# Expert outputs of a two-layer model weighed in feature rows on one core

## The chip, the cores and the metric

The kernel runs on one core of a Trainium2 chip. The metric is the device time of one execution in microseconds (us). A core has TensorE (PE, matrix products into the PSUM memory), VectorE (DVE), ScalarE (ACT), GpSimd (POOL), SyncE (SP, here only a queue of DMAs) and 16 DMA engines. PE, DVE and ACT reach PSUM; POOL works on SBUF alone. Each engine runs its own list of instructions in order and waits on semaphores.

## The reference, cut to what matters

128 images become 65 tokens of 64 features each, and pass two blocks of attention (or recurrence) and a mixture of experts. Each of the two mixtures has 8 experts, of which every token takes two:

```python
combine = sum(topk_probs[..., None] * one_hot(topk_idx, E), axis=-2)      # layer 0
for e in range(E):
    h = relu(einsum('bsd,hd->bsh', x, W1[e]) + b1[e])
    y = einsum('bsh,dh->bsd', h, W2[e]) + b2[e]
    out = out + combine[..., e:e + 1] * y
...
weights = sum(tp[..., None] * one_hot(ti, NE), axis=1)                    # layer 1
for e in range(NE):
    hh = silu(flat @ w1[e].T) * (flat @ w3[e].T)
    out = out + weights[:, e:e + 1] * (hh @ w2[e].T)
```

The attention of layer 1 ends in `x = x + y @ wo.T`, then `x` is added to `h`.

## The kernel before, in words

`h` holds all tokens as [128 images, 65, 64]. `program` runs six phases one after another, with a barrier of all engines between them. Two of them are `moe(0, ...)` and `moe(1, ...)`; the last part of the attention of layer 1, just ahead of `moe(1, ...)`, is `output1`.

`moe` takes the 65 tokens in 13 groups of 5 (`T = 5`, so 640 columns of 5 tokens by 128 images). All experts are computed for all tokens. The first products have feature rows: a unit `u` is one block of 128 hidden features times half a group (320 columns), made of two matmuls in layer 0 (weights in a high and a low part, L1306) and of four in layer 1 (gate and up). Hidden features go from PSUM to `hid` through DVE or ACT (L1079, L1216 in layer 0; L1074 and then L1210 in layer 1). `down` (L1317) multiplies them by the second weights and gives `psY`, 64 features of two experts in 128 rows; ACT's `read_y` copies it to `y[slot][:, p, :]` (L1063, L1065), p = 0 to 3 being the pair of experts.

The order is written out by hand. `body(g, ...)` of each engine walks over places (p, k): pair p and the k-th unit of it, 8 units for each pair in layer 0 and 6, 6, 4, 6 in layer 1. Tables say at which place other work stands: `LOGITS` (router products of group g), `DOWN` (`down` of the pair before), `HI`, `KEEP`, `TURN` (the next group's normalised tokens transposed), `EXP`, and `SLOTS`, steps of DVE's small work: "a" and "e" routing of group g, "n" the norm of group g + 1. PE may run up to four units ahead of their eviction in layer 0 (`wait_evicted(pe, g, u - 4)`); in layer 1 gate products have three PSUM banks. `down(p)` waits for the eviction of all of pair p.

`OUTS` and `WEIGH` place the end of the group before: `token_major` (L1328) turns `y` back to image rows, 4 transposes of 128x128 for each token, 20 for each group. `weigh` on DVE (L1200) multiplies the 512 columns of a token by its 8 routing weights, out of PSUM. POOL's `add_up` adds 512 columns to 64 in three steps (L1001, L1003, L1004) and the sums to `h` (L1006). In layer 1 SP stores each group (L1026).

`output1` has 13 groups too. For each token `yT[:, at:at + B]` is the stationary matrix and `wo1`, 64 columns, moves through it (L1968). DVE adds the product to `x` (L1976) and `x` to `h` (L1979).

## Time and profile before

| | us |
|---|---|
| three runs | 1227.97, 1220.97, 1228.97 |
| median of the runs | 1227.97 |
| profiled execution, its own time | 1219.27 |
| its span, first to last instruction | 1217.5 |
| mean granted clock of TensorE | 0.937 of full speed |

The span is what the rows below divide. Of the profile's rows each names the line of the kernel, the engine, the operation and its tiles; buffer numbers are left out, so `moe_psU` is any of `psU0` to `psU4`. Busy times of PE come from modelled ends and overlap; what counts is how far starts lie apart.

### The profile page before, as it was taken

Reading aid. Unit: us, or ns where it says so; the run is one execution under the profiler, and the core shown is the slowest. Engines: PE = TensorE matmul, PEld = TensorE weight load, DVE = VectorE, ACT = ScalarE, POOL = GpSimd, SP = SyncE. Lnnn points to the kernel's source line nnn. Section 1 sums busy time; section 2 is a strip of 40 time slices with the busy share of each in tenths; the row PEclk is TensorE's granted clock in tenths of the full one; section 3 lists DMA queues with packets and bytes.
Section 4 is the critical chain, followed back from the end, with each engine's and each line's share of the span. In section 5 each row is a group of like instructions: output and inputs, shape, how many; then the busy total and the mean of one; then the engine's idle time right before and its main releaser. Section 6 shows DMA issues by size and latency. Waiting matters only on the chain. (4 is left out here: it accounts for less than half of the span.)

```text
span 1217.5 us, 23980 instructions
## 1 busy us (share of the span) xinstructions
PE 1081.6 (89%) x8420; PEld 811.2 (67%) x8420; DVE 879.7 (72%) x2104; ACT 608.3 (50%) x1269; POOL 458.1 (38%) x613
## 2 busy tenths in 40 slices
PE   6795877959999999997588969988799999999996
PEld 2464776746777777775474547768687777777774
DVE  1696656966777777775678769973677888877874
ACT  2254774636556655653324437770554454554552
POOL 2373001211434434434326478730033433333334
PEclk8797999969999999999698989995799999999998
DMA  8100000000000000000000000000000000000000
GB/s 246 83 1 1 2 1 2 1 1 1 2 1 1 1 1 2 1 1 1 1 1 1 1 1 3 2 3 1 1 7 6 7 6 7 6 12 6 7 7 12
DMA packets 3455, 13.57 MB, mean 11 GB/s; under 512 B 400, under 2 KB 2192, under 8 KB 2960
## 3 DMA queue, kind: packets, MB, share of 16 engines
q1 hardware_dynamic: 3056, 8.00, 2.3%
q0 software_dynamic: 288, 4.11, 0.9%
q8 instruction: 68, 1.11, 0.4%
q14 instruction: 43, 0.35, 0.1%
HBM read 9.97 MB, written 2.13 MB: 10 GB/s over the span
## 5 line engine op out<-in xcount | busy, mean ns | idle before, releaser
L1306 PE MATMUL moe_psU<-moe_nT_parts,moe_w_hi 128*128 128x320 f32 x988 | 325.4, 340 | 1.7 <-ACT moe_nT_parts L1048 0.9
L1306 PE MATMUL moe_psU<-moe_nT_parts,moe_w_lo 128*128 128x320 f32 x988 | 297.4, 311 | 0.0
L1306 PEld LDWEIGHTS moe_psU<-moe_nT_parts,moe_w_hi 128*128 128x128 f32 x988 | 188.5, 191 | 56.6 <-issue 50.1
L1306 PEld LDWEIGHTS moe_psU<-moe_nT_parts,moe_w_lo 128*128 128x128 f32 x988 | 189.1, 191 | 0.0
L1210 DVE TENSOR_TENSOR moe_hid<-moe_psU,moe_silu 128x320 f32<-128x320 f32 x286 | 139.4, 491 | 62.3 <-ACT moe_silu L1074 52.6
L1001 POOL TENSOR_TENSOR moe_sum<-moe_scaled 128x256 f32<-128x256 f32 x130 | 99.1, 763 | 171.1 <-DVE moe_scaled L1200 170.5
L1074 ACT ACTIVATE moe_silu<-moe_psU 128x320 f32<-128x320 f32 x286 | 125.5, 439 | 56.5 <-PE moe_psU L1306 39.2
L1079 ACT ACTIVATE moe_hid<-moe_psU,middle 128x320 f32<-128x320 f32 x260 | 129.5, 528 | 34.1 <-PE moe_psU L1306 31.8
L126 POOL TENSOR_TENSOR moe_stats<-moe_stats,minus_half 128x5 f32<-128x5 f32 x26 | 31.5, 1213 | 274.6 <-DVE moe_stats L1123 274.6
L1216 DVE TENSOR_SCALAR moe_hid<-moe_psU,middle 128x320 f32<-128x320 f32 x156 | 85.7, 550 | 67.5 <-PE moe_psU L1306 66.7
L1317 PE MATMUL moe_psY<-moe_hid,middle 128*64 128x320 f32 x832 | 124.8, 442 | 0.7 <-ACT moe_hid L1079 0.7
L1317 PE MATMUL moe_psY<-moe_hid,late 128*64 128x320 f32 x832 | 123.4, 439 | 0.9 <-DVE moe_hid L1210 0.9
L1200 DVE TENSOR_TENSOR moe_scaled<-moe_psM,moe_weights 128x512 f32<-128x512 f32 x130 | 88.7, 684 | 17.4 <-PE moe_psM L1328 17.1
L1065 ACT COPY moe_y<-moe_psY 128x640 f32<-128x640 f32 x52 | 36.1, 694 | 107.5 <-PE moe_psY L1317 107.5
L1317 PEld LDWEIGHTS moe_psY<-moe_hid,middle 128*64 128x64 f32 x832 | 55.8, 138 | 50.7 <-issue 11.4
L1317 PEld LDWEIGHTS moe_psY<-moe_hid,late 128*64 128x64 f32 x832 | 55.3, 136 | 49.6 <-issue 10.6
L1063 ACT ACTIVATE moe_y<-moe_psY,middle 128x640 f32<-128x640 f32 x52 | 41.4, 797 | 92.8 <-PE moe_psY L1317 92.8
L1806 POOL COPY heads_keys_b<-attention_keys 32x520 f32<-32x520 f32 x64 | 80.0, 1250 | 15.1 <-PE heads_psS L1830 12.8
L1328 PE MATMUL moe_psM<-early,moe_y 128*128 128x128 f32 x520 | 79.3, 276 | 5.4 <-DVE moe_scaled L1200 3.8
L1328 PEld LDWEIGHTS moe_psM<-early,moe_y 128*128 128x128 f32 x520 | 63.5, 141 | 10.4 <-DVE moe_scaled L1200 5.5
L1003 POOL TENSOR_TENSOR moe_sum<-moe_sum 128x128 f32<-128x128 f32 x130 | 60.3, 464 | 23.5 <-POOL moe_sum L1001 23.5
L1929 ACT COPY heads_probT<-heads_psP 65x512 f32<-65x512 f32 x64 | 34.3, 586 | 29.3 <-PE heads_psP L1839 29.3
(301 smaller groups left out, 1982.5 us busy)
## 6 DMA issues: line engine op xcount, KB each, us to landing
images<-in_x SPq DMA_DIRECT2D x8, 576.0 KB, 11.0
late<-in_late POOLq DMA_DIRECT2D x1, 2456.5 KB, 12.5
out_tokens<-h SPq DMA_DIRECT2D x13, 160.0 KB, 1.8
middle<-in_middle POOLq DMA_DIRECT2D x1, 1554.0 KB, 7.4
early<-in_early SPq DMA_DIRECT2D x1, 1042.5 KB, 18.8
early<-in_early SPq DMA_DIRECT2D x1, 80.0 KB, 2.0
```

The lines of the kernel that those rows point to most:

```text
L1001: chain.link(pool.tensor_tensor(sum4[:, t, :], scaled[:, t, 0:4 * D], scaled[:, t, 4 * D:8 * D], ALU.add))
L1003: chain.link(pool.tensor_tensor(sum2[:, t, :], sum4[:, t, 0:2 * D], sum4[:, t, 2 * D:4 * D], ALU.add))
L1063: ins = act.activation(dst, psY, ACT.Identity, bias=late[:, c["b2"]][:, p:p + 1])
L1074: act.activation(sil[bank][:, :], psU[u % 2][:, 0:HALF], ACT.Silu).then_inc(hid_act, 1)
L1079: act.activation(hid[hid_of[u]][:, :], psU[u % 4][:, 0:HALF], ACT.Relu, bias=late[:, c["b1"]][:, k:k + 1]).then_inc(hid_act, 1)
L1200: dve.tensor_tensor(scaled[:, t, :].rearrange("b (e d) -> b e d", e=E), psM[:, bank:bank + E * D].rearrange("b (e d) -> b e d", e=E), weig ...
L1210: dve.tensor_tensor(hid[hid_of[u]][:, :], psU[2 + gate_bank[u]][:, 0:HALF], sil[gate_bank[u]][:, :], ALU.mult).then_inc(hid_dve, 1)
L1216: dve.tensor_scalar(hid[hid_of[u]][:, :], psU[u % 4][:, 0:HALF], late[:, c["b1"]][:, k:k + 1], 0.0, ALU.add, ALU.max).then_inc(hid_dve, 1)
L1306: last = pe.matmul(psum[:, 0:HALF], w[:, col:col + SPLIT], moving, start=(part == 0), stop=(part == 1))
L1317: last = pe.matmul(psY[64 * side:64 * side + 64, half, :], w[:, block_at, :], hid[hid_of[u]][:, :], start=start, stop=stop)
L1328: last = pe.transpose(psM[:, at:at + 128], y[slot][:, p, t * B:(t + 1) * B], ident)
L1806: ins = pool.tensor_copy(kb[i % 2][rows, :, hd, :].rearrange("p b t -> p t b"), by_token(kx)[rows, :, i * BG:(i + 1) * BG])
```

## The change

The routing weights go to the outputs, in feature rows, rather than the outputs to the weights:

1. PE turns the weights of group g - 1 (128x40) in one transpose ahead of the router products of group g (`logits`, line 1346 of the changed kernel). In layer 1 `LOGITS` moves from place (0, 0) to (0, 2).
2. ACT copies them to `weightsT` at place `KEEP_W` (line 1095).
3. SP writes `weightsT` to DRAM (20 KB), waits for it, and reads it back twice, each row repeated over the 64 partitions of an expert, into `wide` (128 x 2560 values, 1.31 MB in two DMAs of 64 partitions; lines 1050 and 1055).
4. DVE multiplies `y` by `wide` in SBUF, once for each pair (`weigh_wide`, 128x640, line 1256), in place of `weigh`.
5. POOL adds the four pairs, three additions of 128x640.
6. In the next body PE turns the sum back, 5 transposes of 128x128 (`back`, line 1396), DVE adds the two halves out of PSUM (`read_back`, line 1264), POOL adds that to `h` (`add_back`).

The last group of each layer keeps the old way, behind the `back` of the group before it. POOL's and SP's loops are written out. `output1` makes `wo1` the stationary matrix, with 512 and 128 columns moving, two groups in the two halves of PSUM; ACT copies, PE turns back with 5 transposes for each pair of groups, DVE adds to `x`, POOL adds `x` to `h`.

```diff
@@ moe, tables of layer 0 and of layer 1
-            OUTS = [(0, 7), (1, 2), (1, 7), (2, 2), (2, 6)]
+            BACK, READ = [(1, 4)], [(1, 6)]
+            WEIGH = [(2, 0), (2, 2), (2, 5), (3, 1)]
-            WEIGH = [(0, 7), (1, 3), (1, 7), (2, 3), (2, 7)]
-            HI, KEEP, EXP = (1, 5), [(3, 2)], (3, 0)
+            KEEP_W, HI, KEEP, EXP = (0, 6), (1, 5), [(3, 2)], (3, 0)
...
-            LOGITS, DOWN = (0, 0), 1
-            OUTS = [(0, 3), (1, 0), (1, 3), (2, 0), (2, 2)]
+            LOGITS, DOWN = (0, 2), 1
+            BACK, READ = [(1, 1), (2, 1)], [(1, 2), (2, 2)]
+            WEIGH = [(1, 4), (2, 0), (2, 3), (3, 0)]
-            WEIGH = OUTS
+            KEEP_W, HI, KEEP, EXP = (0, 4), (1, 3), [(3, 1), (3, 3)], (0, 5)
-            SLOTS = {(0, 1): "aaaannn", (1, 1): "neeeeee", ...
+            SLOTS = {(0, 3): "aaaannn", (1, 1): "neeeeee", ...
@@ POOL
+                def add_back(n):
+                    pool.wait_ge(back_read, PARTS * (n + 1))
+                    tile = resid[:, n * T:(n + 1) * T, :]
+                    pool.tensor_tensor(tile, tile, both[:, :, :], ALU.add).then_inc(added, 1)
...
+                def weigh_wide(n):
+                    mine, into = y[n % 2], total[n % 2]
+                    for p in range(1, PAIRS):
+                        pool.wait_ge(weighed, PAIRS * n + p + 1)
+                        if p == 1:
+                            need(pool, back_mm, PARTS * (n - 1))
+                            chain.link(pool.tensor_tensor(into[:, :], mine[:, 0, :], mine[:, 1, :], ALU.add))
...
@@ SP
+                def widen(n):
+                    sp.wait_ge(wT_set, n + 1)
+                    need(sp, wide_in, 32 * n)
+                    sp.dma_start(scratch.rearrange("e t b -> t e b"), weightsT[:, :]).then_inc(wT_out, 16)
+                    sp.wait_ge(wT_out, 16 * (n + 1))
+                    need(sp, weighed, PAIRS * n)
+                    for side in range(2):
+                        rows = scratch.rearrange("(p s) t b -> s p (t b)", s=2)[side:side + 1]
+                        sp.dma_start(wide[D * side:D * side + D, :, :], rows.to_broadcast([D, PAIRS, TOK])).then_inc(wide_in, 16)
@@ ACT
+                def keep_weights(n):
+                    act.wait_ge(L_mm, n + 2)
+                    act.wait_ge(L_read, n + 2)
+                    need(act, wT_out, 16 * n)
+                    act.copy(weightsT[:, :], weights_ps).then_inc(wT_set, 1)
@@ DVE
+                def weigh_wide(n, p):
+                    dve.wait_ge(wide_in, 32 * (n + 1))
+                    dve.wait_ge(y_out, PAIRS * n + p + 1)
+                    rows = y[n % 2][:, p, :]
+                    dve.tensor_tensor(rows, rows, wide[:, p, :], ALU.mult).then_inc(weighed, 1)
...
+                    halves = psM[:, 0:(t1 - t0) * 128].rearrange("b (t s d) -> b t d s", s=2, d=D)
+                    dve.tensor_reduce(both[:, t0:t1, :], halves, axis=AX.X, op=ALU.add).then_inc(back_read, 1)
@@ PE
+                    if g >= 1:
+                        pe.wait_ge(routed, g)
+                        pe.transpose(weights_ps, weights[:, (g - 1) * T:g * T, :].rearrange("b t e -> b (t e)"), ident)
...
+                def back(n, part):
...
+                    for t in range(t0, t1):
+                        last = pe.transpose(psM[:, (t - t0) * 128:(t - t0 + 1) * 128], total[n % 2][:, t * B:(t + 1) * B], ident)
@@ output1, PE
-                        last = pe.matmul(psW[g % 4][:, t * D:(t + 1) * D], yT[:, at:at + B], late[:, c["wo1"]],
+                    for begin, cols in pieces():
+                        for s in range(n):
+                            at = (g + s) * TOK + begin
+                            last = pe.matmul(psA[k % 2][D * s:D * s + D, begin:begin + cols], late[:, c["wo1"]],
+                                             yT[:, at:at + cols], start=True, stop=True)
```

VectorE in layer 0 before, from the last unit of pair 1 that it evicts, (1, 6), into pair 2:

```order
L1216 TENSOR_SCALAR moe0_hid14<-moe0_psU2,middle 128x320
L1200 TENSOR_TENSOR moe0_scaled<-moe0_psM,moe0_weights 128x512
L1216 TENSOR_SCALAR moe0_hid1<-moe0_psU1,middle 128x320
L1216 TENSOR_SCALAR moe0_hid3<-moe0_psU3,middle 128x320
L1200 TENSOR_TENSOR moe0_scaled<-moe0_psM,moe0_weights 128x512
L1131 TENSOR_TENSOR moe0_split<-moe0_nrm,moe0_split 128x5x64
L856 TENSOR_REDUCE moe0_r_m2<-moe0_r_left 128x5
```

The same stretch in the changed kernel:

```order
L1277 TENSOR_SCALAR moe0_hid14<-moe0_psU2,middle 128x320
L1264 TENSOR_REDUCE moe0_both<-moe0_psM 128x320
L1256 TENSOR_TENSOR moe0_y0<-moe0_y0,moe0_wide 128x640
L1277 TENSOR_SCALAR moe0_hid1<-moe0_psU1,middle 128x320
L1256 TENSOR_TENSOR moe0_y0<-moe0_y0,moe0_wide 128x640
L1277 TENSOR_SCALAR moe0_hid3<-moe0_psU3,middle 128x320
L1180 TENSOR_TENSOR moe0_split<-moe0_nrm,moe0_split 128x5x64
```

The read of the sum and the first two weighings stand ahead of the split; the third weighing follows its six small routing steps, ahead of `hid6`, as L1200 followed `hid6` before.

VectorE in layer 1 before, units (1, 3) to (2, 1):

```order
L1210 TENSOR_TENSOR moe1_hid7<-moe1_psU3,moe1_silu1 128x320
L1210 TENSOR_TENSOR moe1_hid11<-moe1_psU4,moe1_silu2 128x320
L1210 TENSOR_TENSOR moe1_hid0<-moe1_psU2,moe1_silu0 128x320
L1200 TENSOR_TENSOR moe1_scaled<-moe1_psM,moe1_weights 128x512
L1210 TENSOR_TENSOR moe1_hid1<-moe1_psU3,moe1_silu1 128x320
L1131 TENSOR_TENSOR moe1_split<-moe1_nrm,moe1_split 128x5x64
```

And in the changed kernel:

```order
L1271 TENSOR_TENSOR moe1_hid7<-moe1_psU3,moe1_silu1 128x320
L1256 TENSOR_TENSOR moe1_y0<-moe1_y0,moe1_wide 128x640
L1271 TENSOR_TENSOR moe1_hid11<-moe1_psU4,moe1_silu2 128x320
L1271 TENSOR_TENSOR moe1_hid0<-moe1_psU2,moe1_silu0 128x320
L1256 TENSOR_TENSOR moe1_y0<-moe1_y0,moe1_wide 128x640
L1271 TENSOR_TENSOR moe1_hid1<-moe1_psU3,moe1_silu1 128x320
L1180 TENSOR_TENSOR moe1_split<-moe1_nrm,moe1_split 128x5x64
```

The first weighing, which waits for `wide`, now stands ahead of the last eviction of pair 1 (`hid11`).

## Rows read from the trace of the kernel before

**Rows 1.** The page: busy time and share of the span of PE and DVE; the chain that ended last.

```profile
PE 1081.6 (89%) x8420; PEld 811.2 (67%) x8420; DVE 879.7 (72%) x2104; ACT 608.3 (50%) x1269; POOL 458.1 (38%) x613
...
PE moe_psU L1306 15%; PE moe_psY L1317 10%; PE moe_psM L1328 2%; PE moe_psM L1275 1%; PE moe_psM L1283 1%; POOL moe_sum L1001 0%; DVE moe_w_lo L1251 0%; POOL moe_sum L1003 0%; POOL moe_sum L1004 0%; DVE moe_hid L1210 0%; DVE moe_sq L1121 0%; DVE moe_stats L1122 0%; POOL h L1006 0%; ACT moe_y L1065 0%; DVE moe_scaled L1200 0%
```

**Rows 2.** Windows: a body of layer 0, `output1` (two stretches), a body of layer 1.

```profile
core 0: us, PE busy (x) PEld busy (x) DVE busy (x) ACT busy (x) POOL busy (x), PEclk, DMA share, GB/s
400.31:423.77 23.46, 23.46 (x164) 17.37 (x163) 18.04 (x47) 13.85 (x28) 9.94 (x17) 1.00 0.00 1
...
822.00:850.00 28.00, 26.57 (x130) 26.41 (x130) 10.75 (x25) 0.10 (x1) 0.00 (x0) 0.54 0.00 1
...
1000.00:1026.20 26.20, 26.20 (x184) 20.41 (x182) 21.15 (x55) 13.28 (x30) 9.69 (x18) 1.00 0.02 8
```

**Rows 3.** Timeline of PE, layer 0: start, duration, then the instruction.

```profile
399.81 0.31 PE L1306 MATMUL moe_psU<-moe_nT_parts,moe_w_lo 128*128 128x320 f32 x1
399.96 0.60 PE L1328 MATMUL moe_psM<-early,moe_y 128*128 128x128 f32 x4
...
400.54 0.31 PE L1306 MATMUL moe_psU<-moe_nT_parts,moe_w_lo 128*128 128x320 f32 x1
```

**Rows 4.** The same timeline: units (2, 5), (2, 7) and (3, 2).

```profile
422.23 0.42 PE L1306 MATMUL moe_psU<-moe_nT_parts,moe_w_hi 128*128 128x320 f32 x1
...
423.28 0.39 PE L1306 MATMUL moe_psU<-moe_nT_parts,moe_w_hi 128*128 128x320 f32 x1
...
424.25 0.31 PE L1306 MATMUL moe_psU<-moe_nT_parts,moe_w_hi 128*128 128x320 f32 x1
```

**Rows 5.** Timeline of DVE, layer 0: evictions L1216, weighing, split, a routing step.

```profile
417.40 0.55 DVE L1216 TENSOR_SCALAR moe_hid<-moe_psU,middle 128x320 f32<-128x320 f32 x1 [0.16 <-PE moe_psU L1306]
...
420.81 0.48 DVE L1131 TENSOR_TENSOR moe_split<-moe_nrm,moe_split 128x320 f32<-128x320 f32 x1
...
421.43 0.50 DVE L857 TENSOR_TENSOR moe_r_eq<-moe_r_left,moe_r_m 128x40 f32<-128x40 f32 x1
```

**Rows 6.** Timeline of POOL beside it.

```profile
420.97 0.91 POOL L1001 TENSOR_TENSOR moe_sum<-moe_scaled 128x256 f32<-128x256 f32 x1 [0.32 <-DVE moe_scaled L1200]
```

**Rows 7.** Groups by line: POOL's additions, a DVE product of 520 columns in SBUF.

```profile
L1001 POOL TENSOR_TENSOR moe_sum<-moe_scaled 128x256 f32<-128x256 f32 x130 | 99.1, 763 | 171.1 <-DVE moe_scaled L1200 170.5
L1006 POOL TENSOR_TENSOR h<-h,moe_sum 128x320 f32 (+1 forms) x26 | 22.5, 866 | 4.5 <-POOL moe_sum L1004 4.1
L1904 DVE TENSOR_TENSOR heads_prob<-heads_prob,heads_inv 128x520 f32<-128x520 f32 x32 | 23.1, 723 | 1.1
```

**Rows 8.** Issues of DMAs: KB each, median us to landing.

```profile
images<-in_x SPq DMA_DIRECT2D x8, 576.0 KB, 11.0
late<-in_late POOLq DMA_DIRECT2D x1, 2456.5 KB, 12.5
out_tokens<-h SPq DMA_DIRECT2D x13, 160.0 KB, 1.8
```

**Rows 9.** The eight image loads (ns, first and last issue); POOL's two loads; landing of the images.

```profile
L193 SPq DMA_DIRECT2D images<-in_x x8: 413/426/740, 1.2 to 5.0; - x8
...
24.62 0.73 POOL L202 DMA_DIRECT2D middle<-in_middle  x1 [16.68 <-DMA early<-in_early]
25.36 0.54 POOL L203 DMA_DIRECT2D late<-in_late  x1
...
DMA to landing us min/median/max: 4.9/11.0/17.0
```

**Rows 10.** Timeline of ACT, layer 0: evictions (0, 5) and (0, 7).

```profile
411.52 0.94 ACT L1079 ACTIVATE moe_hid<-moe_psU,middle 128x320 f32<-128x320 f32 x2
```

**Rows 11.** Timeline of PE, layer 0, a `down` at half clock.

```profile
275.56 3.72 PE L1317 MATMUL moe_psY<-moe_hid,middle 128*64 128x320 f32 x16
```

**Rows 12.** Timelines of DVE and PE, layer 1: eviction (1, 4), `down` of pair 1.

```profile
1003.35 0.49 DVE L1210 TENSOR_TENSOR moe_hid<-moe_psU,moe_silu 128x320 f32<-128x320 f32 x1
...
1005.26 2.37 PE L1317 MATMUL moe_psY<-moe_hid,late 128*64 128x320 f32 x16
```

More of the change, by code:

```diff
@@ L881, in over_bodies, with moe @@
             chain.leave(1)
-def moe(nc, layer, late, early, src, resid, out, minus_half):
+def moe(nc, layer, late, early, src, resid, out, minus_half, scratch):
     c, ec = columns(LATE if layer else MIDDLE)[0], columns(EARLY)[0]
@@ L939, in moe @@
         scaled = sb("scaled", [B, T, E * D])
+        weightsT, wide = sb("weightsT", [T * E, B]), sb("wide", [128, PAIRS, TOK])
+        total, both = [sb(f"total{k}", [128, TOK]) for k in range(2)], sb("both", [B, T, D])
         sum4, sum2, sum1 = sb("sum4", [B, T, 4 * D]), sb("sum2", [B, T, 2 * D]), sb("sum1", [B, T, D])
@@ L1084, in body @@
                         evict(g, u)
+                        if before and (p, k) == KEEP_W:
+                            keep_weights(g - 1)
                         if layer == 1 and front and (p, k) == KEEP[0]:
@@ L1224, in body @@
                         evict(g, u)
-                        if before:
-                            for t in range(T):
-                                if WEIGH[t] == (p, k):
-                                    weigh(g - 1, t)
+                        if before and (p, k) in WEIGH:
+                            weigh_wide(g - 1, WEIGH.index((p, k)))
+                        if g >= 2 and (p, k) in READ:
+                            read_back(g - 2, READ.index((p, k)))
                         for kind in SLOTS.get((p, k), ""):
@@ L1260, in _ @@
                 chain.leave(1)
+                for part in range(PARTS):
+                    read_back(NT - 2, part)
                 for t in range(T):
@@ L1344, in body @@
                                 down(g - 1, PAIRS - 1)
-                        if before:
-                            for t in range(T):
-                                if OUTS[t] == (p, k):
-                                    if t == 0:
-                                        pe.wait_ge(L_read, g + 1)
-                                    token_major(g - 1, 1 - slot, t)
+                        if g >= 2 and (p, k) in BACK:
+                            back(g - 2, BACK.index((p, k)))
                         if layer == 0 and front and (p, k) == TURN[0]:
@@ L1360, in _ @@
                 down(NT - 1, PAIRS - 1)
+                for part in range(PARTS):
+                    back(NT - 2, part)
                 for t in range(T):
@@ new lines, in turn @@
+                def turn(k):
+                    rows = D * PAIRS[k][1]
+                    pe.wait_ge(sides_set, k + 1)
+                    need(pe, x_set, k - 1)
+                    for t in range(T):
+                        last = pe.transpose(psB[k % 2][:, t * 128:t * 128 + rows], sides[k % 2][0:rows, t * B:(t + 1) * B],
+                                            ident[0:rows, 0:rows])
+                    last.then_inc(B_mm, 1)
+                project(0)
+                for k in range(1, NPAIR):
+                    project(k)
+                    turn(k - 1)
@@ L1972, in _ @@
+                turn(NPAIR - 1)
+            @block.scalar
+            def _(act):
+                for k in range(NPAIR):
+                    rows = D * PAIRS[k][1]
+                    act.wait_ge(A_mm, k + 1)
+                    need(act, B_mm, k - 1)
+                    act.copy(sides[k % 2][0:rows, :], psA[k % 2][0:rows, 0:TOK]).then_inc(sides_set, 1)
             @block.vector
             def _(dve):
-                for g in range(NT):
-                    dve.wait_ge(W_mm, g + 1)
-                    dve.tensor_tensor(flat(x, g), flat(x, g), psW[g % 4][:, 0:T * D], ALU.add).then_inc(x_set, 1)
-                    if g > 0:
-                        dve.wait_ge(x_set, g)
-                        dve.tensor_tensor(flat(h, g - 1), flat(h, g - 1), flat(x, g - 1), ALU.add).then_inc(h_set, 1)
@@ L1999, in program @@
             if phases > 2:
[L2000 removed]
+                moe(nc, 0, middle, early, h, h, None, minus_half, scratch)
         if phases > 3:
@@ L2005, in program @@
         if phases > 5:
-            moe(nc, 1, late, early, n_all, h, out, minus_half)
+            moe(nc, 1, late, early, n_all, h, out, minus_half, scratch)
 def resize_matrix(n):
```

119 lines of the change are left out of this document (76 added, 43 removed).

## The prediction

> **What bounds the kernel now.** I read the page first, then windows over single bodies, then the timelines of each engine in one body. In the page PE is busy 89% of the span and DVE 72%, and the chain that ended last is almost all `moe` on PE: the units and `down` [rows 1]. The windows show the same more sharply: in a body of layer 0 (23.46 us) and of layer 1 (26.20 us) PE has no gap and its clock is full, and DVE is busy 18.0 and 21.2 us of them [rows 2]. So each microsecond that PE is spared in a body counts, as long as DVE keeps up, and DVE has 5 us to spare in each. `output1` is another case: 28 us at a granted clock of 0.54, with PE busy throughout and DVE at 10.8 us [rows 2].
>
> **What PE is spared.** A low-part matmul starts at 399.81, four transposes of `token_major` follow, and the next low-part matmul starts at 400.54. Two steps of 0.147 us between matmuls would make 400.10, so four transposes cost 0.44 us, 0.11 each [rows 3]. A body drops 20 and gets 5 (`back`) and 1 (weights): 14 fewer, 1.54 us. Groups 0 to 11 of both layers change, 24 bodies: 24 x 1.54 = **-37.0 us**. Bodies would take 21.92 and 24.66 us.
>
> **When `wide` is there.** This chain is new: ACT's copy of the weights, SP, a store to DRAM, SP, two loads, DVE. In the old body ACT's evictions of (0, 5) and (0, 7) begin at 411.52 [rows 10]; the copy stands between them, 0.11 us later through the transpose of the weights, so it ends near 411.52 + 0.11 + 0.42 + 0.27 = 412.3 (the same clock as the rows of layer 0; 0.27 for a small copy is an estimate below any copy of 128 columns or more). The store is smaller than a store of an output group, which lands in 1.8 us [rows 8]; SP's wakings I put at 0.2 us each. The loads move 1.31 MB. The trace holds no broadcast. Its nearest rows are two: `middle` and `late` together, 4.11 MB issued from 24.62 on and landed at 25.36 + 12.5 = 37.9 us, which without 2 us of fixed time is 365 GB/s and gives 2.0 + 3.6 = 5.6 us; and the images, of which the first lands 4.9 us after issue and the last at 5.0 + 17.0 = 22.0, seven of 590 KB in 15.9 us, 260 GB/s, which gives 2.3 + 5.0 = 7.3 us [rows 8, 9]. I take 5.6, the lower end, since both together fill all partitions as `late` does, and keep 7.3. The chain is 0.2 + 1.8 + 0.2 + 5.6 + 0.2 = 8.0 us (up to 9.7): `wide` is there at 420.3 (up to 422.0).
>
> **Layer 0, the wait and what stands behind it.** Ahead of the first weighing DVE evicts (1, 6) and reads the sum back. The eviction starts at 417.40 in the old body [rows 5]; two groups of four transposes are gone by then and 6 single ones came, so it starts near 417.18. An eviction takes 0.47 us of DVE's time from start to start. A product of 520 columns in SBUF takes 0.72 us and DVE starts the next 0.08 earlier [rows 7], so I put `read_back` and each `weigh_wide` (640 columns) at 0.74. DVE is at the first weighing at 418.4 and waits 1.9 us. Queued behind it are, in this order: eviction (2, 1), second weighing, eviction (2, 3), split, six routing steps (1.45 us), third weighing, eviction (2, 6). PE needs (2, 1) for unit (2, 5), (2, 3) for (2, 7) and (2, 6) for (3, 2), four units ahead. In the new body without any stall those start at 421.13, 421.74 and 422.71 (from 422.23, 423.28 and 424.25) [rows 4].
>
> A second thing slows DVE. The routing step at 421.43, a product of 40 columns, takes 0.50 us instead of its usual 0.20, and ends just as POOL's addition of 0.91 us from 420.97 does, at 421.9; other such steps in the trace do the same [rows 5, 6]. So a DVE operation with two inputs in SBUF waits for a POOL addition under way. Those additions were 0.76 us at 256 columns and 0.87 at 320 [rows 7]; at 640 I put them at 1.55. The first is started by the second weighing, just ahead of the split, which has two such inputs.
>
> Walk: weighing 420.30 to 421.04; (2, 1) done 421.6 (PE late by 0.5); weighing to 422.25; (2, 3) done 422.8 (PE late by 1.1); POOL adds from 422.35 to 423.9, the split ends its slot at 424.3; routing steps to 425.75; weighing to 426.5; (2, 6) done 427.05. Unit (3, 2) starts 4.4 us late. In pairs 3 and 0 DVE has no weighing but one and catches up. **Layer 0: +4.4 us a body.** Without POOL's lock it would be 3.1; with the lock and `wide` in time 2.9; with neither 1.25, since pair 2 simply holds more of DVE's work than before.
>
> **Layer 1** the same way. From the copy of the weights behind (0, 4) to DVE's eviction of (1, 4) lie six units of 0.59 us, a `down` of 2.3 and four transposes, 6.5 us with the eviction itself; the chain takes 8.0, so DVE waits 1.5. The eviction of (1, 5), which `down` of pair 1 needs, is now behind the weighing. In the old body eviction (1, 4) starts 1.91 us ahead of that `down` [rows 12]; less 0.44 of transposes that is 1.47. Behind it now come 0.45 of eviction, 1.5 of wait, 0.74 and 0.5, 3.2 us: `down` is late by about 1.85. Then the lock holds the split by 1.2 us, which costs 0.45 at (3, 1), and the fourth weighing by 0.75, which with seven routing steps makes (3, 2) late by 1.25 for PE's third gate bank. **+3.5 us a body**; 1.85 without the lock, 2.0 with the lock and `wide` in time, 0 with neither. `logits` now waits for `routed`, which DVE signals with over 1 us to spare; the copy on ACT (0.3 us a body) is hidden in its idle time.
>
> **`output1`.** Per pair of groups PE streams 1280 columns and then transposes five times. Sixteen passes of 320 columns take 2.3 us at full clock [rows 12] and 3.7 at half [rows 11]; with two passes for each product, a pair costs 1.15 + 0.55 = 1.7 or 1.86 + 1.1 = 3.0. Six and a half pairs are 11 or 19 us, filling and draining (first product, ACT, turn, DVE 0.8, POOL 1.55) 3.5. The stage takes 14.5 to 23 us instead of 28. Its clock was low and PE will stream denser; I take 18.5, **-9.5 us**.
>
> **Tails.** After the last body `back` and `read_back` of group 11 now stand ahead of `token_major`: 0.55 + 0.9 us, each layer: **+3 us**. Everything else is unchanged.
>
> **Sum.** -37.0 + 12 x (4.4 + 3.5) - 9.5 + 3 = +51.3, from 1219.3 to 1270.6 us for the profiled execution. That lies 8.7 us under the median and 1.7 under the lowest of three; for a median I add half of the distance and get 1275.
>
> **Rivals.** (a) *DVE comes late to `wide` anyway and PE keeps its lead*: the loads land before 418.4 and the lock does nothing. For it: DVE's idle 5 us a body, and that the locked steps of before were short. Against: it needs a chain under 6.1 us, less than one store and one load by the rows. Then 12 x (1.25 + 0) = 15, in all -28.5: 1191 + 4 = 1195; with nothing lost at all 1180. This ends faster; it decides whether DVE shows a wait for `wide`. (b) *Only one of lock and late loads*: 12 x (3.1 + 1.85) or 12 x (2.9 + 2.0), both +59, in all +16: 1239. (c) *The loads are slower, since each fills only half of the partitions and the second queues behind the first*: `late`, over all 128, had 365 GB/s, the images, over 96, 260. At the images' rate the chain is 1.7 us longer, and once DVE is late each microsecond counts in all 24 bodies: +41, 1316.
>
> By the Trainium skill, page "SBUF — State Buffer", section "Door 1: The DMA port swizzle", 64 partitions from one end reach half of the ports, and two DMAs to the two halves gain only 6% over one; it measured 196 GB/s for a 1 MiB transfer of 64 partitions. By that the loads would take about 8.7 us and the kernel about 1350, an estimate. No load of 64 partitions is in this trace, so it neither bears that out nor denies it; the two measured rates have the same order, the images' tiles of 96 partitions being the slower.
>
> **Chances.** Forecast (1250 to 1300) 0.46; (a) 0.27; (b) 0.14, of which half is within 1%; (c) 0.13. Three runs spread by 0.65%, so about 1% is what a measurement can tell from no change. Faster by over 1% 0.27, within 1% 0.10, slower 0.63. The range leaves out the best of (a) and the worst of (c), 0.1 each: 1192 to 1316.
>
> **What would show it.** Right: DMAs to `wide` that land 7 to 10 us after ACT's copy, DVE idle before line 1256 until a DMA for 1.5 to 4 us in every body, PE idle until `moe_hid` at (3, 2) and at `down` of pair 1, bodies of about 26 and 28 us; split and the fourth weighing stretched beside POOL's additions; `output1` under 20 us. Wrong: bodies of 22 and 24.7 us with no idle PE. If PE's gaps also bring its granted clock down, the loss is larger than summed.

## The result, and the profile after

The kernel after takes 1413.0 us (median, 1400.4 to 1415.9) against 1228.5: 1.149 times as long (95% interval 1.142 to 1.157). The prediction had the sign, but 1413 lies far above its 1275 and outside its range of 1192 to 1316. The profiled run has a span of 1398.6 us, 181 more than before.

The page of the kernel after: busy time, the chain that ended last (by engine, by line), one group and one issue. They answer to [rows 1] and [rows 8].

```profile
PE 1112.4 (80%) x8041; PEld 791.9 (57%) x8041; DVE 915.3 (65%) x2097; ACT 618.7 (44%) x1300; POOL 403.1 (29%) x332
...
PE 14%; DMA 9%; DVE 7%; issue 2%; ACT 1%; SPq 1%; POOL 0%; DVEq 0%; ACTq 0%; POOLq 0%
...
L1256 DVE TENSOR_TENSOR moe_y<-moe_y,moe_wide 128x640 f32<-128x640 f32 x96 | 104.2, 1085 | 94.3 <-DMA moe_wide<-routing_weights 94.3
...
moe_wide<-routing_weights SPq DMA_DIRECT2D x48, 640.0 KB, 7.5
```

PE has 379 matmuls fewer and yet is busy longer; the chain is no longer PE's alone, and DVE waits 94 us for `wide`.

Windows of the kernel after, as in [rows 2]: two bodies of layer 0, two together of layer 1.

```profile
417.23:447.23 30.00, 25.33 (x146) 17.05 (x145) 19.55 (x45) 14.01 (x30) 6.67 (x5) 0.89 0.21 45
476.17:506.17 30.00, 24.13 (x146) 16.41 (x145) 19.31 (x46) 14.01 (x30) 6.69 (x6) 0.94 0.21 45
1072.00:1142.90 70.90, 58.16 (x336) 41.99 (x336) 45.24 (x108) 26.73 (x62) 14.89 (x10) 0.88 0.20 43
```

The mean of the ten full bodies is 30.2 us in layer 0 (predicted 26.3) and 34.8 in layer 1 (28.2), and the granted clock of these windows is 0.88 to 0.94 where [rows 2] have 1.00. Both losses are in each body, so one body tells the story. Timeline of SP, ACT, DVE, POOL and PE in the layer 0 body from 417.23 (the rows of each engine in order of time):

```profile
417.82 0.75 SPq L1050 DMA_DIRECT2D routing_weights<-moe_weightsT  x1
419.85 1.25 SPq L1055 DMA_DIRECT2D moe_wide<-routing_weights  x2
```

```profile
417.55 0.25 ACT L1095 COPY moe_weightsT<-moe_psM 40x128 f32<-40x128 f32 x1
```

```profile
423.35 0.82 DVE L1264 TENSOR_REDUCE moe_both<-moe_psM 128x320 f32<-128x640 f32 x1
428.51 0.82 DVE L1256 TENSOR_TENSOR moe_y<-moe_y,moe_wide 128x640 f32<-128x640 f32 x1 [4.34 <-DMA moe_wide<-routing_weights]
...
430.91 1.65 DVE L1180 TENSOR_TENSOR moe_split<-moe_nrm,moe_split 128x320 f32<-128x320 f32 x1
...
435.37 1.54 DVE L1256 TENSOR_TENSOR moe_y<-moe_y,moe_wide 128x640 f32<-128x640 f32 x1
```

```profile
430.66 1.54 POOL L1017 TENSOR_TENSOR moe_total<-moe_y 128x640 f32<-128x640 f32 x1 [5.54 <-issue]
434.68 1.55 POOL L1019 TENSOR_TENSOR moe_total<-moe_total,moe_y 128x640 f32<-128x640 f32 x1 [2.48 <-DVE moe_y L1256]
```

```profile
429.85 0.63 PE L1372 MATMUL moe_psU<-moe_nT_parts,moe_w_hi 128*128 128x320 f32 x1 [2.63 <-DVE moe_hid L1277]
435.05 0.41 PE L1372 MATMUL moe_psU<-moe_nT_parts,moe_w_hi 128*128 128x320 f32 x1 [2.04 <-DVE moe_hid L1277]
...
436.76 3.92 PE L1383 MATMUL moe_psY<-moe_hid,middle 128*64 128x320 f32 x16
```

The copy ends at 417.80 and DVE gets `wide` at 428.51: a chain of 10.7 us, not 8.0. From the copy to the issue of the loads it takes 2.05 us (summed: 2.2); from there to DVE 8.66 instead of 5.6 and a wake. DVE stands still for 4.34 us. Beside POOL's additions (1.54, as predicted) the split takes 1.65 us instead of 0.48 [rows 5] and a weighing 1.54 instead of 0.82. PE has two gaps of 4.7 us together, and `down` behind them takes 3.92 us instead of 2.37 [rows 12]. Windows of the gaps and of what follows each show the granted clock:

```profile
427.22:429.85 2.63, 0.00 (x1) 0.00 (x0) 1.34 (x3) 0.79 (x1) 0.00 (x0) 0.97 0.02 4
429.85:432.85 3.00, 3.00 (x10) 2.60 (x10) 2.96 (x5) 1.39 (x3) 1.54 (x1) 0.50 0.00 0
432.85:435.05 2.20, 0.16 (x1) 0.00 (x0) 2.06 (x8) 0.40 (x2) 0.37 (x1) 0.94 0.01 4
436.76:440.60 3.84, 3.84 (x17) 1.63 (x16) 2.82 (x8) 0.64 (x2) 1.53 (x1) 0.59 0.00 0
```

Behind the first gap the units run at a granted clock of 0.50, the lower of its two levels, and `down` behind the second has 0.59 as a mean. So PE is busy 25.3 us for the work that takes it 22.4 at full clock (experiment 4).

In layer 1 `add_back` stands ahead of the sums in POOL's order, and three additions follow each other at once. Timelines of POOL, of DVE and of PE in the layer 1 body from 1107.91:

```profile
1124.79 0.88 POOL L1007 TENSOR_TENSOR h<-h,moe_both 128x320 f32<-128x320 f32 x1 [15.71 <-DVE moe_both L1264]
1125.74 2.01 POOL L1017 TENSOR_TENSOR moe_total<-moe_y 128x640 f32<-128x640 f32 x1
1127.83 2.04 POOL L1019 TENSOR_TENSOR moe_total<-moe_total,moe_y 128x640 f32<-128x640 f32 x1
1129.94 1.54 POOL L1021 TENSOR_TENSOR moe_total<-moe_total,moe_y 128x640 f32<-128x640 f32 x1
```

```profile
1117.48 0.82 DVE L1256 TENSOR_TENSOR moe_y<-moe_y,moe_wide 128x640 f32<-128x640 f32 x1 [3.02 <-DMA moe_wide<-routing_weights]
...
1125.02 1.32 DVE L1256 TENSOR_TENSOR moe_y<-moe_y,moe_wide 128x640 f32<-128x640 f32 x1
...
1126.67 1.77 DVE L1256 TENSOR_TENSOR moe_y<-moe_y,moe_wide 128x640 f32<-128x640 f32 x1
...
1128.76 1.16 DVE L1233 SCALAR_TENSOR_TENSOR moe_r_val<-moe_r_prob,moe_r_eq 128x40 f32<-128x40 f32 x1
...
1130.19 1.36 DVE L1235 TENSOR_TENSOR moe_r_first<-moe_r_first,moe_r_val 128x40 f32<-128x40 f32 x1
```

```profile
1118.85 4.06 PE L1383 MATMUL moe_psY<-moe_hid,late 128*64 128x320 f32 x16 [3.55 <-DVE moe_hid L1271]
...
1132.89 0.64 PE L1372 MATMUL moe_psU<-moe_nT_parts,moe_w_hi 128*128 128x320 f32 x1 [2.28 <-DVE moe_hid L1271]
```

Four operations of DVE take 5.6 us beside the additions that take 0.82 or 0.20 elsewhere (2.0), and PE waits 2.3 us for DVE behind them. Its larger gap, 3.55 us, is at `down` of pair 1, whose last eviction stands behind DVE's wait for `wide` (3.02 us).

For the comparisons below a body is the distance between two steps of POOL at line 126, one in each body (417.23 and 447.25 for the one above). Where bodies vary I give the mean of ten, else the value at which they stay.

### The profile page after: what moved, and what is told of

The parts are those of the page before. It is cut to its first block and busy times, and to the rows that moved or that the text cites. A ratio compares the mean times of both kernels' runs of the same rounds, so it can differ in the third digit from the quotient of the medians.

```text
span 1398.6 us, 22565 instructions
## 1 busy us (share of the span) xinstructions
PE 1112.4 (80%) x8041; PEld 791.9 (57%) x8041; DVE 915.3 (65%) x2097; ACT 618.7 (44%) x1300; POOL 403.1 (29%) x332
## 5 line engine op out<-in xcount | busy, mean ns | idle before, releaser
L1372 PE MATMUL moe_psU<-moe_nT_parts,moe_w_hi 128*128 128x320 f32 x988 | 341.0, 355 | 104.8 <-DVE moe_hid L1277 65.2
L1372 PE MATMUL moe_psU<-moe_nT_parts,moe_w_lo 128*128 128x320 f32 x988 | 311.7, 325 | 0.0
L1372 PEld LDWEIGHTS moe_psU<-moe_nT_parts,moe_w_lo 128*128 128x128 f32 x988 | 200.2, 203 | 0.0
L1383 PE MATMUL moe_psY<-moe_hid,late 128*64 128x320 f32 x832 | 149.6, 510 | 44.7 <-DVE moe_hid L1271 44.7
L1256 DVE TENSOR_TENSOR moe_y<-moe_y,moe_wide 128x640 f32<-128x640 f32 x96 | 104.2, 1085 | 94.3 <-DMA moe_wide<-routing_weights 94.3
L1383 PEld LDWEIGHTS moe_psY<-moe_hid,late 128*64 128x64 f32 x832 | 67.9, 159 | 106.0 <-issue 77.6
L126 POOL TENSOR_TENSOR moe_stats<-moe_stats,minus_half 128x5 f32<-128x5 f32 x26 | 31.5, 1211 | 278.6 <-DVE moe_stats L1172 278.6
L1007 POOL TENSOR_TENSOR h<-h,moe_both 128x320 f32<-128x320 f32 x24 | 20.9, 873 | 275.8 <-DVE moe_both L1264 275.8
L1017 POOL TENSOR_TENSOR moe_total<-moe_y 128x640 f32<-128x640 f32 x24 | 42.5, 1770 | 88.5 <-issue 57.9
L1019 POOL TENSOR_TENSOR moe_total<-moe_total,moe_y 128x640 f32<-128x640 f32 x24 | 42.4, 1769 | 33.7 <-DVE moe_y L1256 32.8
L1339 PE MATMUL moe_psM<-early,moe_split 128*128 128x128 f32 x130 | 25.3, 320 | 19.4 <-DVE moe_split L1180 18.5
## 6 DMA issues: line engine op xcount, KB each, us to landing
images<-in_x SPq DMA_DIRECT2D x8, 576.0 KB, 11.6
```

The source lines that it names most:

```text
L1017: chain.link(pool.tensor_tensor(into[:, :], mine[:, 0, :], mine[:, 1, :], ALU.add))
L1019: chain.link(pool.tensor_tensor(into[:, :], into[:, :], mine[:, 2, :], ALU.add))
L1256: dve.tensor_tensor(rows, rows, wide[:, p, :], ALU.mult).then_inc(weighed, 1)
L1372: last = pe.matmul(psum[:, 0:HALF], w[:, col:col + SPLIT], moving, start=(part == 0), stop=(part == 1))
L1383: last = pe.matmul(psY[64 * side:64 * side + 64, half, :], w[:, block_at, :], hid[hid_of[u]][:, :], start=start, stop=stop)
```

## The experiments

Theories after the result. **T**: the loads of `wide` come 3 us later than summed, since they fill half of the partitions each; POOL's additions hold DVE; PE's gaps bring the clock down, and the three add up. Rivals: one of the two alone is nearly all; or the loss comes from elsewhere, such as `output1` or PE itself.

**1. `output1` alone.** The kernel before with the new function and its call:

```diff
-        output1(nc, late, h, x, nT)
+        output1(nc, late, early, h, x, nT)
```

> The kernel before, with the new output1 alone; both moe phases as before. Theory: the stage gains what its window showed, 28.2 to 17.9 us, and nothing follows it: 1228 - 10 = 1218 us. Rival 1, the stage ends sooner but the clock of the phase behind it starts lower, so that moe gives half of it back: 1223. Rival 2, the whole loss of 185 us begins here, by a bad state that output1 leaves for the last phase: over 1300.

Measured: 1210.9 us, 0.988 of before (0.983 to 0.993). The first step of layer 1 on POOL starts at 841.14 instead of 853.17, and the bodies keep 26.19 us: 12.0 us gained (9.5 predicted), nothing given back. This is the fastest of the versions that do all the work, faster than both kernels.

**2. Loads once.**

```diff
+                    if n > 0:
+                        return
                     for side in range(2):
...
```

> The kernel after, with the two wide loads issued for the first group of each layer alone; later groups are weighed by the first group's weights, the stores of the weights go on. So wide is always in time and POOL's additions stay. Theory (late loads, POOL's lock and the clock behind PE's gaps each carry a part, the loads the largest): the waits for the DMA of 3 to 4.3 us a body go, and most of the half-clock stretches with them: bodies of about 26 and 28.5, 1184 + 12 x (4.0 + 4.0) = 1280 us. Rival 1, late loads are nearly all of it: 1195 to 1215. Rival 2, DVE is held by POOL's additions whatever the loads do: over 1350.

Measured: 1296.4 us, 1.057 (1.047 to 1.067). Bodies of 24.16 and 30.5 us. The lateness is 117 of the 185 us; layer 0 is left 1.2 us above the kernel before, layer 1 still 4.3 us. One load in each layer is still late, in the body that follows the first group (30.66 us in layer 0, 32.34 in layer 1).

**3. Small additions.**

```diff
-    pool.tensor_tensor(into[:, :], mine[:, 0, :], mine[:, 1, :], ALU.add)
+    pool.tensor_tensor(into[:, 0:8], mine[:, 0, 0:8], mine[:, 1, 0:8], ALU.add)
... (the other two additions in the same way)
```

> The kernel after, with POOL's three additions of a group cut to 8 of their 640 columns (the rest of the sum is left out); the loads stay late. Theory: the stretched operations of DVE (split 1.65 in place of 0.48, a weighing of 1.77 in place of 0.82, routing steps of 1.2 and 1.4 in place of 0.2) return to their usual times, 2.5 us a body in layer 0 and 3.6 in layer 1, but the waits for the DMA stay: 1413 - 12 x (2 + 4) = 1341 us, down to 1320 by the clock. Rival 1, the late loads hide the lock's price: 1390 to 1413. Rival 2, the lock is the larger of the two: under 1290.

Measured: 1345.5 us, 1.099 (1.090 to 1.107), 68 us less than after; bodies of 28.1 and 31.4 us. Both single rivals fall, late loads alone and lock alone.

**4. Both.**

> Both at once: loads for the first group alone and additions of 8 columns. Theory: what is left is the spared transposes, the new output1, DVE's crowding and the moved logits: 1228 - 37 - 10 + 3 + 12 x (1.25 + 1.0) = 1211 us. If the two together are all of the loss, 1184 to 1190. Rival (something else costs too, such as the store, the copy on ACT, or the order of POOL's steps): over 1240.

Measured: 1233.1 us, 1.005 (1.000 to 1.009). 180 us go, the sum of 117 and 68 within the error: the two causes add up. But 1233 is not the 1211 that was expected. Of these 22 us 11.6 are the one late load left in each layer (bodies of 30.05 and 31.01 us in place of 22.98 and 26.47). The rest is in the bodies themselves: they stay at 22.98 us in layer 0, just as before, though 14 transposes are gone, and at 26.47 in layer 1 (26.19 before). The windows of one body each show it:

```profile
388.93:411.91 22.98, 22.42 (x146) 15.34 (x144) 16.69 (x46) 13.57 (x30) 3.15 (x6) 1.00 0.01 2
1051.70:1078.17 26.47, 25.01 (x170) 19.00 (x170) 20.09 (x56) 13.33 (x32) 3.12 (x5) 1.00 0.03 9
```

PE has gaps of 0.56 and 1.46 us now, each time waiting for an eviction of DVE; 1.03 of the 1.46 stand in one gap early in the body, where in layer 1 the routing and the norm now fall together. A third loss shows only in starts. Timeline of PE in the same kernel, where no transpose stands any more:

```profile
404.98 0.31 PE L1375 MATMUL moe_psU<-moe_nT_parts,moe_w_hi 128*128 128x320 f32 x1
405.13 0.30 PE L1375 MATMUL moe_psU<-moe_nT_parts,moe_w_lo 128*128 128x320 f32 x1
405.38 0.41 PE L1375 MATMUL moe_psU<-moe_nT_parts,moe_w_hi 128*128 128x320 f32 x1
405.63 0.30 PE L1375 MATMUL moe_psU<-moe_nT_parts,moe_w_lo 128*128 128x320 f32 x1
```

and its weight load of the third row:

```profile
405.38 0.19 PEld L1375 LDWEIGHTS moe_psU<-moe_nT_parts,moe_w_hi 128*128 128x128 f32 x1 [0.20 <-ACT moe_hid L1129]
```

Steps of 0.147 become 0.25 twice: by its row the weight load waited for ACT's eviction of an earlier unit. Before, four transposes stood in such places.

**5. Fewer transposes, nothing else**, to price that term:

```diff
-                    for p in range(PAIRS):
+                    for p in range(1):
...
```

> The kernel before, with 5 of the 20 transposes of a body in token_major (pairs 1 to 3 are left out of the result; DVE's weighings and POOL's additions keep their size and places, and the output is as before). It prices the spared transposes by themselves, 15 a body. By the prediction's 0.11 us each: 1.65 us a body in 26 bodies, 1228 - 43 = 1185 us. Theory after the run without loads and without additions, whose layer 0 body is 22.98 us as before although 14 transposes are gone: PE waits for evictions of psU in their place. Then layer 0 gains 0 to 0.3 us a body and layer 1 about 1: 1228 - 13 x 1.2 = 1212 us. Rival: nothing in either layer, 1228.

Measured: 1198.1 us, 0.975 (0.971 to 0.979). Its windows, one body of each layer:

```profile
388.50:410.40 21.90, 21.90 (x147) 15.23 (x145) 17.44 (x46) 13.37 (x28) 9.75 (x18) 1.00 0.00 1
1000.00:1024.58 24.58, 24.58 (x170) 18.81 (x167) 20.98 (x56) 13.18 (x30) 9.65 (x18) 1.00 0.02 8
```

15 transposes are worth 1.07 us in layer 0 (0.07 each) and 1.61 in layer 1 (0.11 each). Both forecasts miss: the gain is there, smaller in layer 0 than the prediction's and larger than the theory's. So in experiment 4 the gain was there, and 1.0 us in layer 0 and 1.8 in layer 1 were lost again elsewhere.

**6. Loads by pair.** Four DMAs of 128 partitions in place of two of 64, each weighing waits for its own:

```diff
+    for p in range(PAIRS):
+        rows = scratch[2*p:2*p+2].rearrange("s t b -> s (t b)").unsqueeze(1).to_broadcast([2, D, TOK])
+        sp.dma_start(wide[:, p, :], rows).then_inc(piece_in[p], 16)
...
```

> The kernel after, with wide loaded by four DMAs, one for each pair (128 partitions, 0.33 MB each) instead of two for the two halves of the partitions (0.66 MB each); DVE waits for the piece of its pair. Theory (the two loads are slow because each has half of the partitions and the second stands behind the first, and the first weighing needs both): the first piece is there about 3.5 us after its issue, the last after 6 to 7, so DVE's 94 us of waits for the DMA fall under 20: near the kernel that loads once, 1296 us, up to 1320. Rival 1, the broadcast itself is slow, 1.31 MB in 5.5 us or more whatever its shape: the last piece lands 8 us or more after the first issue; the first weighing is early, a later one waits: 1340 to 1370. Rival 2, four issues of 0.6 us on SP and small pieces give it all back: 1400.

Measured: 1663.5 us, 1.353 (1.347 to 1.358), worse than any expectation. Timelines of SP and of DVE, layer 0:

```profile
439.46 11.55 SPq L1057 DMA_DIRECT2D moe_wide<-routing_weights  x4
```

```profile
405.08 0.82 DVE L1258 TENSOR_TENSOR moe_y<-moe_y,moe_wide 128x640 f32<-128x640 f32 x1 [4.70 <-DMA moe_wide<-routing_weights]
411.56 0.83 DVE L1258 TENSOR_TENSOR moe_y<-moe_y,moe_wide 128x640 f32<-128x640 f32 x1 [5.20 <-DMA moe_wide<-routing_weights]
418.03 0.83 DVE L1258 TENSOR_TENSOR moe_y<-moe_y,moe_wide 128x640 f32<-128x640 f32 x1 [2.38 <-DMA moe_wide<-routing_weights]
```

A piece of 0.33 MB comes every 6.5 us, 50 GB/s. SP's four issues take 11.55 us together instead of 1.25 for two; single ones take 0.79 us as a median and up to 10.5. The last columns of a window over these loads are the share of the 16 DMA engines that is busy, and GB/s:

```profile
400.00:418.00 18.00, 6.26 (x32) 3.81 (x30) 5.58 (x12) 4.05 (x9) 2.41 (x2) 0.74 0.13 51
```

The outermost dimension of the source is 2 here (a side) where it was 64. By the Trainium skill, page "DMA: Bandwidth & Descriptors", section "Rules for kernel authors", an outermost dimension of c below 16 confines a DMA to at most c engines; the trace agrees: a share of 0.13 is two of 16 engines. The run says nothing on T; it shows what the shape of a broadcast can cost.

**7. The first addition ahead of `add_back`** in layer 1:

```diff
+                    if g >= 1:
+                        weigh_wide(g - 1, range(1, 2))
                     if g >= 2:
                         add_back(g - 2)
...
```

> The kernel after, with POOL's first addition of layer 1 ahead of add_back in POOL's order, so that the three additions don't all stand behind read_back. Theory (in layer 1 the additions run back to back for 5.7 us since the first waits behind add_back, and hold two weighings and two routing steps for 3.6 us in all): with one of them 5 us earlier, beside DVE's waits for evictions, the body of 34.9 us falls by 1 to 2 us: 1413 - 18 = 1395 us. Rival: the additions hold DVE as long wherever they stand: 1405 to 1415.

Measured: 1393.6 us, 1.133 (1.129 to 1.138), 19 us less; layer 1's body falls by 1.5 us to 33.3. As expected.

**8. The weights turned early.** The transpose of the weights leaves `logits` and stands behind unit (0, 0):

```diff
+                        if before and (p, k) == (0, 0):
+                            turn_weights(g - 1)
...
-            KEEP_W, HI, KEEP, EXP = (0, 6), (1, 5), [(3, 2)], (3, 0)
+            KEEP_W, HI, KEEP, EXP = (0, 1), (1, 5), [(3, 2)], (3, 0)
...
```

> The kernel after, with the transpose of the weights taken out of logits and put behind unit (0, 0), its copy on ACT at (0, 1) in layer 0 and (0, 0) in layer 1, and in layer 0 logits one place later for ACT's copy. The chain to wide keeps its length and starts 3 to 4 us earlier in layer 0 and 4 to 5 in layer 1. Theory: DVE's waits for the DMA (3 to 4.3 us a body) go nearly to nothing, and this kernel, which does all the work, comes near the one that loads once: 1296 to 1320 us. Rival 1, the loads hold something else (DVE's own reads of SBUF, ACT, PE) while they run, which the kernel that loads once didn't show: 1340 to 1370. Rival 2, PE now waits for the routing weights instead, as these come 3 us after the old place in a body: 1350 or more.

Measured: 1283.3 us, 1.044 (1.039 to 1.049), bodies of 24.1 and 30.6. The chain is as long as ever (the loads land 5.5 to 8.7 us after issue) and DVE's wait for it falls from 94.3 to 0.8 us. All work is done, so 130 of the 185 us are the chain's end and what hangs on it. That is more than the 117 of experiment 2, where one load in each layer stayed late.

**9. One load over 128 partitions:**

```diff
-                    for side in range(2):
-                        rows = scratch.rearrange("(p s) t b -> s p (t b)", s=2)[side:side + 1]
-                        sp.dma_start(wide[D * side:D * side + D, :, :], rows.to_broadcast([D, PAIRS, TOK])).then_inc(wide_in, 16)
+                    rows = scratch.rearrange("(p s) t b -> s p (t b)", s=2)[0:1]
+                    sp.dma_start(wide[:, :, :], rows.to_broadcast([128, PAIRS, TOK])).then_inc(wide_in, 16)
```

> The kernel after, with wide loaded by one DMA over all 128 partitions, outermost dimension 128, the same 1.31 MB in the same rows of 2.5 KB; both halves get the weights of the even experts (the odd experts are weighed wrongly). Theory (a DMA into 64 partitions reaches half of what one into 128 does, and the second of the two queues behind the first): the load lands 5 to 6 us after its issue instead of 8.6 for the pair, DVE's waits for the DMA fall from 94 us to about 30, the kernel to about 1330. Rival 1, the rate of about 200 GB/s is the broadcast's own, whatever the partitions: it lands 8 us after its issue and only the second issue of 0.6 us is spared: 1395 to 1410. Rival 2, slower than the pair: over 1415.

Measured: 1315.2 us, 1.070 (1.063 to 1.076). Its page, the issue (KB, median us to landing), and the same row of experiment 10:

```profile
moe_wide<-routing_weights SPq DMA_DIRECT2D x24, 1280.0 KB, 5.9
```

```profile
moe_wide<-routing_weights SPq DMA_DIRECT2D x24, 640.0 KB, 5.7
moe_wide<-routing_weights ACTq DMA_DIRECT2D x24, 640.0 KB, 6.0
```

Twice the bytes land in the same time once all 128 partitions take part: 5.9 us against 5.7 for one half alone, and 8.66 for both halves. Windows over the loads while their bytes move, first the kernel after, then this one:

```profile
421.80:427.00 5.20, 5.20 (x37) 3.62 (x34) 1.28 (x2) 3.27 (x7) 0.87 (x1) 1.00 1.05 224
440.60:443.60 3.00, 3.00 (x21) 2.58 (x19) 1.28 (x2) 2.75 (x6) 0.54 (x1) 1.00 0.98 362
```

All 16 engines are busy in both, so it isn't engines that the two halves lack: busy as they are, they move 224 GB/s there and 362 here. DVE's waits are 27.4 us. This run is the one that the prediction had assumed, with a chain of 8 us: bodies of 27.3 and 30.8 us where it said 26.3 and 28.2. A window of one body of layer 0:

```profile
436.04:463.20 27.16, 24.07 (x146) 16.47 (x145) 19.22 (x46) 13.89 (x30) 6.68 (x5) 0.94 0.15 50
```

**10. The second half issued by ACT**, on the kernel of experiment 8:

```diff
+                    act.dma_start(wide[D:2 * D, :, :], rows.to_broadcast([D, PAIRS, TOK])).then_inc(wide_in, 16)
```

> The kernel with the early turn of the weights, with the load of the upper half of wide issued by ACT (behind its eviction of (0, 7) in layer 0, (0, 3) in layer 1) instead of SP. The loads are off the path there, so the landings are what is looked at. Theory (both loads share the engines and ports, the queue is not what orders them): the pair still takes 6.5 to 7 us from the first byte to the last, each load 7 to 8 us. Rival (they were one behind the other on SP's queue and could run side by side): both land within 5.5 to 6 us of their issue. Time: 1283 us plus what ACT's issue of 0.6 us a body costs its evictions, 1283 to 1300.

Measured: 1281.5 us (1.044, 1.034 to 1.054), no change. In a body of layer 0 SP issued at 453.22 and ACT only at 455.88, and by the medians above they land 5.7 and 6.0 us after their own issue. Between the issues lie 2.66 us, and with each load's first part, in which no bytes move, the transfers hardly overlapped, so whether the queue or the ports put one behind the other stays open.

**11. Repaired.** Experiments 7 and 8 together, with layer 1's `logits` back at (0, 0):

```diff
-            LOGITS, DOWN = (0, 2), 1
+            LOGITS, DOWN = (0, 0), 1
```

> The kernel with the early turn, and in layer 1 also logits back at (0, 0) with the turn of the weights just ahead of unit (0, 0), and POOL's first addition ahead of add_back. It does all the work. Layer 0 stays at its 24.1 us a body. Theory for layer 1's 30.6 us, which lie 4.4 above those of before although 14 transposes are gone: the move of logits to (0, 2) costs 1.8 us (routing steps and norm fall together at (0, 3)) and the additions in a row 1.5: a body of 27.3 us and 1283 - 12 x 3.3 = 1243 us. Rival 1, the move of logits cost nothing and only the order of the additions counts: 1265. Rival 2, PE waits for the copy of the weights ahead of logits: 1275 or more.

Measured: 1259.3 us, 1.028 (1.021 to 1.036), between the theory's 1243 and rival 1's 1265; layer 1's body 28.35 as a mean, 1.8 less than in experiment 8 (30.2 as a mean), not 3.3.

**12. Repaired, small additions.**

> The same kernel with POOL's three additions cut to 8 of 640 columns (the rest of the sum is left out). Nothing is late, nothing is locked, logits are where they were. Theory: layer 0 as in the run without loads and additions, 22.98 us; layer 1 24.9: 12 x (24.9 - 26.2) = -16, output1 -12, first bodies and tails +8, so 1228 - 20 = 1208 us, below output1 alone by 3. Rival (what layer 1 loses besides lateness and lock is not the moved logits): 1225 to 1235.

Measured: 1200.9 us, 0.976 (0.968 to 0.983); bodies of 22.93 and 25.21. Against experiment 4 layer 1's body is 1.26 us shorter with `logits` back in place. The two kernels differ in more (the early turn, the loads of every group, POOL's order), but layer 0's body is the same in both to 0.05 us, and PE's gap of 1.03 us in layer 1 is gone, so most of the 1.26 is the move. Here a part of the prediction's gain is real, but the sum is not made: 58 us lie between this and experiment 11. Even so layer 0 gains nothing over the kernel before (22.93 against 22.97), layer 1 1.0 us a body.

**13. The additions on DVE**, on the kernel of experiment 11:

```diff
+                        first = mine[:, 0, :] if p == 1 else into[:, :]
+                        dve.tensor_tensor(into[:, :], first, mine[:, p, :], ALU.add).then_inc(
...
```

> The repaired kernel with the three additions of a group done by DVE, each right behind the weighing of its pair, in place of POOL. It does all the work. Theory (the price is POOL's lock: an operation of DVE that meets an addition waits for up to 1.2 us, four or five times a body): DVE takes on 3 x 0.8 = 2.4 us a body of work and loses the lock, which in the repaired kernel filled 3.0 us of DVE's windows in layer 0 and as much in layer 1; PE sees less of it, since the work stands evenly: bodies of 23.5 and 26.5 us instead of 24.1 and 28.2, 1259 - 12 x 2.3 = 1231 us. Rival 1, the work as such counts, not who does it: 1255 to 1265. Rival 2, DVE becomes the bound, as it has the evictions behind each addition: over 1270.

Measured: 1256.3 us, 1.023 (1.015 to 1.031), equal to experiment 11 in total. The routing step that took 1.16 us beside an addition takes 0.19 again:

```profile
1124.88 0.19 DVE L1233 SCALAR_TENSOR_TENSOR moe_r_val<-moe_r_prob,moe_r_eq 128x40 f32<-128x40 f32 x1
```

Bodies are 25.5 us in layer 0, worse than with POOL (24.4), and 26.7 in layer 1, better (28.35). So the stretching is POOL's lock and goes with it, but what it costs is about what 2.5 us of DVE's own work cost. In layer 0 bodies of 24.7 us at a granted clock of 1.00 alternate with bodies of 26.3 at 0.94; at full clock throughout, the two kernels' bodies are 24.7 and 24.1, so half of the difference there is the clock. Rival 1 held in the sum, T in layer 1.

## Why the prediction was wrong

The failing step is *when `wide` is there*. It took 5.6 us for the loads, "since both together fill all partitions as `late` does". They don't move at the rate of `late`: it is 8.66 us from the first issue to DVE. Experiment 9 removes just that and gives back 98 us of the 138 by which the prediction missed. The two profiled runs are 80.4 us apart (1398.6 and 1318.2): PE's idle time falls by 62.3 (286.2 to 223.9) and its busy time by 18.1 (1112.4 to 1094.3) for the same 8041 matmuls, with a granted clock of 0.925 instead of 0.901. The Trainium skill, page "SBUF — State Buffer", section "Door 1: The DMA port swizzle", gave an estimate of 8.7 us for the loads in the prediction, and the trace agrees: 8.66. The prediction quoted it and kept it out of its range; its own rival (c), slower halves one behind the other, priced the lateness with the images' rate, 1.7 us where 3 was right. (By its own rows the first image of 0.59 MB takes 2.3 us of its 4.9 at 260 GB/s, which leaves 2.6 us of fixed time and not the 2.3 of the sum, and makes the 1.7 a 2.1.) That the halves are slow is shown; whether one stands behind the other isn't.

The second term is *the clock*. It was named as a risk and put at nothing in the sum. PE's busy time at equal work is 33 us more in experiment 9 than in experiment 4 (1094.3 and 1061.0), where the granted clock of a body is 1.00. That is most of the other 40 us. A body of layer 1 with and without the additions' lock (experiments 2 and 4; that of 4 is shown there) shows it too:

```profile
1038.62:1069.23 30.61, 26.90 (x168) 19.56 (x168) 22.82 (x56) 13.32 (x31) 7.62 (x5) 0.94 0.02 7
```

PE is busy 26.90 us here and 25.01 there. What a gap costs behind it isn't a constant: between experiment 4 and the kernel after PE's idle time grows by 118 us and its busy time by 51, between experiments 12 and 11 its idle time by 43 and its busy time by only 4.

By the steps of the prediction, from the bodies of experiment 9, whose 1.0 us too much in layer 0 and 2.6 in layer 1 make 43 us in 12 bodies each, less 2.5 for `output1`:

- *PE spared*: 1.54 a body predicted; by experiment 5, 14 transposes are 1.0 in layer 0 and 1.5 in layer 1. The 0.11 of [rows 3] took steps of 0.147 for granted in their place. 7 us over both layers.
- *Layer 0*, +4.4: 27.3 - 21.98 = 5.3 measured. Three parts: with neither lateness nor lock 1.25 predicted, 1.0 measured (experiment 12 against 5), of which 0.55 is a gap of PE that waits for DVE in pair 2, as predicted, and the rest slower steps, which were not. The lock with the loads in time: 1.65 predicted, 1.2 measured (24.16 against 22.98). The lateness of a chain of 8 us on top: 1.5 predicted, 3.1 measured (27.3 against 24.16), of which PE's idle time is 1.4 and its busy time, by the clock, 1.6. So the idle time was right and the clock was missing.
- *Layer 1*, +3.5: 30.8 - 24.7 = 6.1 measured. With neither lateness nor lock 0 predicted, 1.8 measured, most of it the move of `logits`, which was priced at nothing. The lock with the loads in time: 2.0 predicted, 4.0 measured (30.5 against 26.47), of which 1.9 is the clock. The lateness on top: 1.5 predicted, 0.3 measured. For the lock the walk had looked at POOL's additions one by one, not at POOL's order: `add_back` waits for the second `read_back` and makes the additions fall in a row beside DVE's last weighings and routing steps; experiment 7 gets 1.5 us a body back by that order alone.
- With the loads as late as they were, the lock costs 2.1 us in layer 0 and 3.4 in layer 1 (the kernel after against experiment 3), where 1.3 and 1.65 were predicted.
- *`output1`*: -9.5 predicted, -12.0 measured. *ACT's copy* (0.25, 0.27 predicted), *store to DRAM* (2.05 us from the copy to the next issue, 2.2 predicted), *additions* (1.54, 1.55 predicted), `read_back` and weighings (0.74 from start to start, as predicted): right.

The walk by due times itself held: the places of PE's gaps in layer 0, (2, 5) and (3, 2), are those it named, and from `wide` to the start of (3, 2) it had 6.75 us where 6.54 were measured (428.51 to 435.05). With `wide` 2.7 us later still the gaps are 2.6 and 2.0 us instead of 0.5 and 3.3 at these two places, the second shorter because the units between them run at the lower clock and fill a part of it. Why experiment 11 gains 1.8 us in layer 1 where the parts alone give 1.3 and 1.5 stays open.

## What to carry to other kernels

A new chain through memory in a loop must be timed by a row of the same shape: a load into 64 partitions is no half of a load into 128. Where it can be started earlier, do that first; here it was worth 130 us, more than any change of the loads. Before moving work off PE, ask what PE would do in the places that come free, and write down each engine's order around a wait, since what stands behind the waiting instruction falls in a heap later. Give a risk that is named a price: the clock, put at nothing, was 33 us of PE's busy time. Take the parts of such a change apart: `output1` alone was the gain.
